# Another cyclic order of the first layer's work on five engines of a fused two-layer attention kernel

## What is computed

```python
x = x + _L0_xattn_ref(_layernorm(x), ctx_1024, ...)  # 16 heads of 8
x = x + _L0_ffn_ref(_layernorm(x), ...)  # 8 experts, top 2
x = x + _L1_xattn_ref(_layernorm(x), ctx_1024, ...)  # 16 heads of 64
x = x + _L1_ffn_ref(_layernorm(x), ...)
```

## Time and profile before

| | us |
|---|---|
| median of 3 runs | 1002.3 (1001.92 to 1004.87) |
| time of the profiled execution | 1007.77 |
| its span, first to last instruction | 1006.1 |
| PE busy (matmuls) | 918.5 (91%) |
| DVE busy | 670.3 (67%) |
| ACT busy | 580.7 (58%) |
| mean granted TensorE clock | 0.962 |

### The profile page before, as it was taken

How to read it: one execution, slowest core, us unless ns; L and a number is a source line. 1 busy time by engine, 2 the same in 40 slices (tenths; PEclk the granted TensorE clock), 3 DMA queues, 4 the chain that set the end, 5 groups by cost and what they waited for, 6 DMA issues and landing times. The chain is left out here.

```text
span 1006.1 us, 30348 instructions
## 1 busy us (share of the span) xinstructions
PE 918.5 (91%) x8590; PEld 800.9 (80%) x8590; DVE 670.3 (67%) x2173; ACT 580.7 (58%) x2537; POOL 414.3 (41%) x670
## 2 busy tenths in 40 slices
PE   4989989899899729999948999999999999999986
PEld 2667767677677529999947899999999999999976
DVE  5778979898699742222226777777777777777763
ACT  1978979899699603332305565556555555555552
POOL 4123434344344421111134555555555555555441
PEclk9999999999899959999978999999999999999998
DMA  4685576756667122222211111111121111111110
GB/s 151 208 247 160 192 228 195 231 191 206 188 197 222 61 69 68 73 68 68 73 55 39 53 54 46 63 57 48 51 63 57 51 48 63 57 43 56 60 48 9
DMA packets 110659, 103.58 MB, mean 103 GB/s; under 512 B 11759, under 2 KB 96563, under 8 KB 110614
## 3 DMA queue, kind: packets, MB, share of 16 engines
q1 hardware_dynamic: 102958, 89.14, 28.5%
q0 software_dynamic: 5776, 12.99, 4.1%
q10 hardware_dynamic: 1880, 0.92, 0.3%
HBM read 56.45 MB, written 46.56 MB: 102 GB/s over the span
## 5 line engine op out<-in xcount | busy, mean ns | idle before, releaser
L590 ACT ACTIVATE PR<-bank,nmx 128x128 f32<-128x128 f32 x1024 | 363.5, 384 | 114.6 <-issue 109.2
L590 ACT ACTIVATION_READ_ACCUMULATOR PR<-bank,nmx 128x1 f32 x1024 | 229.4, 224 | 0.0
L757 DVE TENSOR_REDUCE nmx<-bank 128x4 f32<-128x512 f32 x256 | 168.7, 680 | 35.6 <-PE bank L1051 28.1
L328 POOL TENSOR_TENSOR PR<-PR,rden 128x512 f32<-128x512 f32 x128 | 133.8, 1045 | 88.9 <-DVE rden L762 87.9
L1033 PEld LDWEIGHTS bank<-ident,PR 128*128 128x128 f32 x1024 | 119.9, 142 | 42.8 <-issue 39.4
L1033 PE MATMUL bank<-ident,PR 128*128 128x128 f32 x1024 | 150.1, 277 | 1.0 <-DVE YT L768 1.0
L1212 PE MATMUL bank<-XCT,wqk 128*128 128x128 f32 x1024 | 123.6, 280 | 0.9 <-ACT XCT L582 0.9
L1212 PEld LDWEIGHTS bank<-XCT,wqk 128*128 128x128 f32 x1024 | 120.4, 197 | 1.6 <-ACT XCT L582 1.6
L658 ACT ACTIVATE H<-bank 128x512 f32<-128x512 f32 x70 | 41.8, 597 | 107.0 <-PE bank L1182 107.0
L288 POOL TENSOR_SCALAR veps<-mv 128x1 f32<-128x1 f32 x128 | 28.6, 223 | 181.7 <-DVE mv L304 167.2
L582 ACT ACTIVATE XCT<-bank 128x256 f32<-128x256 f32 x64 | 24.6, 384 | 128.0 <-PE bank L1025 127.7
(11 more groups left out here) (180 smaller groups left out, 1834.1 us busy)
## 6 DMA issues: line engine op xcount, KB each, us to landing
second_layer_values<-wide SPq DMA_DIRECT2D x32, 512.0 KB, 3.3
wide<-second_layer_values SPq DMA_DIRECT2D x32, 512.0 KB, 3.3
expert_outputs<-HF SPq DMA_DIRECT2D x32, 256.0 KB, 2.6
expert_outputs<-HF SPq DMA_DIRECT2D x64, 128.0 KB, 1.9
KBD<-expert_outputs SPq DMA_DIRECT2D x128, 64.0 KB
QS<-expert_outputs SPq DMA_DIRECT2D x32, 256.0 KB
PR<-expert_inputs SPq DMA_DIRECT2D x36, 128.0 KB, 2.0
expert_outputs<-PR POOLq DMA_DIRECT2D x35, 128.0 KB, 2.0
```

The costliest lines, as they stand in the source:

```text
L328: nc.gpsimd.tensor_tensor(unit, unit, rden[:, p, G * g:G * g + G].unsqueeze(2).broadcast_to([P, G, P]), ALU.mult).then_inc(s["nm"], 1)
L590: last = nc.scalar.activation(PR[:, g, j * P:(j + 1) * P], S_BANK[g % 2][:, j * P:(j + 1) * P], ACT.Exp, bias=nmx[:, p, h:h + 1], accum_ou ...
L757: nc.vector.tensor_reduce(nmx[:, p, G * g:G * g + G], S_BANK[g % 2][:].rearrange("p (j k) -> p j k", j=G), AXX, ALU.max, negate=True).then ...
```

## The change

The same instructions are issued in another cyclic order on PE, DVE and ACT, two swaps are made on SP and POOL, and each step is cut at another place, so that late loads and the ends of the pipeline fall elsewhere. With both orders written from V on, in the old numbering of n:

- **PE before**: V(n-2), T1(n-1), transpose of n-3, T2(n-1), o(n-2), S0(n), v0(n), cnt(n-4), transpose of n+2, S1(n), pj0(n+1), T3(n-1), KQ(n+2), RB(n-1), lg(n-3), S2(n), pj1(n+1), T0(n), S3(n).
- **PE after**: V(n-2), S0(n), transpose of n-3, T1(n-1), o(n-2), v0(n), pj0(n+1), S1(n), transpose of n+2, T2(n-1), cnt(n-4), T3(n-1), S2(n), KQ(n+2), RB(n-1), pj1(n+1), T0(n), lg(n-3), S3(n). Its step is now cut ahead of T3, and two more steps are unrolled at the start (`behind` 6 for 4).
- **DVE before**: chosen, ql(n+1), XDT, stats(n+3), x(n-2), reciprocal, M0(n), place and next, M1(n), P2(n-1), stats(n-2), picked, slots, lgs, max, placed, KC to QC(n+2), M2(n), max_index, norm(n-2), tope and hot, M3(n), P0(n), norm(n+3), oN(n-1).
- **DVE after**: ql(n+1), M0(n), XDT, reciprocal, chosen, x(n-2), stats(n-2), stats(n+3), M1(n), place and next, P2(n-1), picked, M2(n), KC to QC(n+2), slots, norm(n+3), placed, lgs, norm(n-2), max, M3(n), max_index to hot, P0(n), oN(n-1).
- **ACT before**: copy of n+2, E0(n), pjv0(n+1), E1(n), P3(n-1), pjv1(n+1), RTS(n-1), E2(n), qh(n+2), E3(n), P1(n), copy vc(n+1).
- **ACT after**: E0(n), copy of n+2, vc(n), pjv0(n+1), E1(n), P3(n-1), E2(n), RTS(n-1), qh(n+2), pjv1(n+1), E3(n), P1(n).
- **SP before**: context(n+3), KBD(n+1), QS(n+1), kw(n+2), store of values(n+1), qw(n+2); loads between loops come ahead of context(n+3).
- **SP after**: QS(n), kw(n+1), store of values(n), context(n+3), early loads, qw(n+1), KBD(n+1); loads between loops come ahead of QS(n). In the cycle only the context and early loads have moved, from behind qw to ahead of it; the late loads have moved from ahead of context and KBD to between KBD and QS.
- **POOL**: the copy XK of n-3 goes behind the two norms.

```diff
@@ -393,32 +393,32 @@
 
             def step0(n, p):
                 q = 1 - p
+                if exists(n):
+                    wait_apart(sp, (a["qw"], 32 * (n + 1)), (a["s"], NU * (n - 1)))
+                    sp.dma_start(QS[:, p, :, :].bitcast(FP32),
+                                 spread(p, 0).rearrange("(g x) s -> x g s", g=NU)).then_inc(a["qs"], 16)
+                if exists(n + 1):
+                    wait_apart(sp, (a["kl"], n + 2), (a["bd"], 16 * G * (n)))
+                    sp.dma_start(spread(q, 1).rearrange("(c o i) s -> c o i s", o=2, i=2),
+                                 PARTS[:, 0:2, :].unsqueeze(1).broadcast_to([P, 2, 2, P])).then_inc(a["kw"], 16)
+                if exists(n):
+                    wait_apart(sp, (a["pjv"], 2 * (n + 1)))
+                    sp.dma_start(v_dram[n], V_OUT).then_inc(a["vst"], 16)
                 if exists(n + 3):
                     load_ctx(sp, a, n + 3, q)
                 if isinstance(n, int):
                     early_loads(n)
                 if exists(n + 1):
+                    wait_apart(sp, (a["ql"], n + 2), (a["qs"], 16 * (n)))
+                    for o in range(2):
+                        sp.dma_start(spread(q, 0).rearrange("(c o i) s -> o c i s", o=2, i=2)[o],
+                                     PARTS[:, 2 + o, :].unsqueeze(1).broadcast_to([P, 2, P])).then_inc(a["qw"], 16)
                     if isinstance(n, int) and n + 1 < 2:
                         sp.wait_ge(bd_zeroed, n + 2)
                     wait_apart(sp, (a["kw"], 16 * (n + 2)), (a["s"], NU * (n)))
                     for j in range(G):
                         rows = spread(q, 1).rearrange("(g j x) s -> j x g s", g=NU, j=G)[j]
                         sp.dma_start(KBD[32 * j:32 * j + 32, q, :, j, :].bitcast(FP32), rows).then_inc(a["bd"], 16)
-                    wait_apart(sp, (a["qw"], 32 * (n + 2)), (a["s"], NU * (n)))
-                    sp.dma_start(QS[:, q, :, :].bitcast(FP32),
-                                 spread(q, 0).rearrange("(g x) s -> x g s", g=NU)).then_inc(a["qs"], 16)
-                if exists(n + 2):
-                    wait_apart(sp, (a["kl"], n + 3), (a["bd"], 16 * G * (n + 1)))
-                    sp.dma_start(spread(p, 1).rearrange("(c o i) s -> c o i s", o=2, i=2),
-                                 PARTS[:, 0:2, :].unsqueeze(1).broadcast_to([P, 2, 2, P])).then_inc(a["kw"], 16)
-                if exists(n + 1):
-                    wait_apart(sp, (a["pjv"], 2 * (n + 2)))
-                    sp.dma_start(v_dram[n + 1], V_OUT).then_inc(a["vst"], 16)
-                if exists(n + 2):
-                    wait_apart(sp, (a["ql"], n + 3), (a["qs"], 16 * (n + 1)))
-                    for o in range(2):
-                        sp.dma_start(spread(p, 0).rearrange("(c o i) s -> o c i s", o=2, i=2)[o],
-                                     PARTS[:, 2 + o, :].unsqueeze(1).broadcast_to([P, 2, P])).then_inc(a["qw"], 16)
                 if isinstance(n, int) and n == -2:
                     sp.wait_ge(rows_zeroed, 1)
                     sp.wait_ge(parts_ready, 1)
@@ -518,15 +518,15 @@
                     nc.gpsimd.tensor_copy(RB[:].rearrange("p (t k d) -> p k t d", t=2, k=PAIRS),
                                           rden[:, q, :].rearrange("p (k t) -> p k t", k=PAIRS).unsqueeze(3)
                                           .broadcast_to([P, PAIRS, 2, DH0])).then_inc(a["rb"], 1)
-                if exists(n - 3):
-                    wait_apart(pool, (rt["xn"], n - 2), *([(rt[f"sc{q}"], 2 * loads(n - 5, q))] if exists(n - 5) else []))
-                    nc.gpsimd.tensor_copy(XK[:, q, :], XND[:]).then_inc(rt["kept"], 1)
                 if exists(n - 2):
                     norm_pool(pool, rt, n - 2, p)
                 if exists(n + 3):
                     norm_pool(pool, a, n + 3, q)
                 if isinstance(n, int):
                     late_constants(n)
+                if exists(n - 3):
+                    wait_apart(pool, (rt["xn"], n - 2), *([(rt[f"sc{q}"], 2 * loads(n - 5, q))] if exists(n - 5) else []))
+                    nc.gpsimd.tensor_copy(XK[:, q, :], XND[:]).then_inc(rt["kept"], 1)
                 if exists(n - 4):
                     for k in range(2):
                         wait_apart(pool, (rt["placed"], n - 3), (rt["kept"], n - 3))
@@ -606,36 +606,36 @@
 
             def step0(n, p):
                 q = 1 - p
+                if exists(n + 1):
+                    act.wait_ge(a["qc"], n + 2)
+                    wait(act, a["qw"], 32 * (n + 1))
+                    nc.scalar.activation(PARTS[:, 2, :].bitcast(FP32R), QC, ACT.Copy).then_inc(a["qh"], 1)
+                if exists(n):
+                    read_v_half(n, 1)
+                if exists(n - 1):
+                    exponentials(a, n - 1, q, 3)
+                    read_PT(a, n - 1, 1)
...
+                if exists(n):
+                    exponentials(a, n, p, 0)
                 if exists(n + 2):
                     read_xct(a, n + 2, p, True, a["v0"], n + 1)
                 if exists(n):
-                    exponentials(a, n, p, 0)
+                    act.wait_ge(a["v0"], n + 1)
...
+                    nc.scalar.activation(diagonal(p), bank[4][:, 2 * P:3 * P].rearrange("p (k t d) -> p k t d", k=PAIRS, t=2),
+                                         ACT.Copy).then_inc(a["vc"], 1)
                 if exists(n + 1):
                     read_v_half(n + 1, 0)
                 if exists(n):
                     exponentials(a, n, p, 1)
                 if exists(n - 1):
                     read_PT(a, n - 1, 3)
-                if exists(n + 1):
-                    read_v_half(n + 1, 1)
+                if exists(n):
+                    exponentials(a, n, p, 2)
                 if exists(n - 1):
                     act.wait_ge(a["rt"], n)
                     wait(act, a["oN"], n - 1)
                     nc.scalar.activation(RTS[:], M2_BANK[:, 2 * P:3 * P], ACT.Copy).then_inc(a["rts"], 1)
-                if exists(n):
-                    exponentials(a, n, p, 2)
-                if exists(n + 2):
-                    act.wait_ge(a["qc"], n + 3)
...
-                    nc.scalar.activation(PARTS[:, 2, :].bitcast(FP32R), QC, ACT.Copy).then_inc(a["qh"], 1)
-                if exists(n):
-                    exponentials(a, n, p, 3)
-                    read_PT(a, n, 1)
-                if exists(n + 1):
-                    act.wait_ge(a["v0"], n + 2)
...
-                    nc.scalar.activation(diagonal(q), bank[4][:, 2 * P:3 * P].rearrange("p (k t d) -> p k t d", k=PAIRS, t=2),
-                                         ACT.Copy).then_inc(a["vc"], 1)
             over_steps(act, step0, -3, NB + 3, 3, 4)
@@ -772,55 +772,63 @@
                 q = 1 - p
                 if isinstance(n, int):
                     weights_and_masks(n)
+                if exists(n - 1):
+                    row_max(a, n - 1, q, 3)
                 if exists(n - 4):
-                    wait(dve, rt["hot"], n - 3)
-                    nc.vector.tensor_tensor(chosen[:], hot1[:, 0, :], hot1[:, 1, :], ALU.add).then_inc(rt["chosen"], 1)
...
+                    wait_apart(dve, (rt["top8"], n - 3))
+                    nc.vector.max_index(topi[:], top8[:], lgs[:]).then_inc(rt["topi"], 1)
...
+                if exists(n - 1):
+                    read_PT(a, n - 1, 0)
+                if exists(n - 2):
...
+                    nc.vector.tensor_tensor(OT0[:, p, :], O_BANK, RTS[:], ALU.mult).then_inc(a["oN"], 1)
+                if exists(n):
+                    row_max(a, n, p, 0)
+                if exists(n - 1):
+                    nc.vector.reciprocal(rden[:, q, :], den[:, q, :]).then_inc(a["rd"], 1)
+                if exists(n - 4):
+                    wait(dve, rt["hot"], n - 3)
+                    nc.vector.tensor_tensor(chosen[:], hot1[:, 0, :], hot1[:, 1, :], ALU.add).then_inc(rt["chosen"], 1)
+                if exists(n - 2):
+                    nc.vector.tensor_tensor(xrow, M2_BANK[:, 0:P], xrow, ALU.add).then_inc(a["x"], 1)
+                    norm_alone_stats(dve, rt, a["x"], n - 2)
                 if exists(n + 3):
                     norm_dve_stats(dve, a, None, n + 3, q)
-                if exists(n - 2):
-                    nc.vector.tensor_tensor(xrow, M2_BANK[:, 0:P], xrow, ALU.add).then_inc(a["x"], 1)
-                if exists(n - 1):
-                if exists(n):
-                    row_max(a, n, p, 0)
+                if exists(n):
+                    row_max(a, n, p, 1)
...
-                if exists(n):
-                    row_max(a, n, p, 1)
-                if exists(n - 2):
-                    norm_alone_stats(dve, rt, a["x"], n - 2)
...
-                    nc.vector.tensor_reduce(slot_f[:, :, bass.ds(n - 4, 1)].rearrange("p k o -> p (k o)"), picked[:], AXX,
...
-                    dve.wait_ge(rt["lg"], n - 2)
-                    nc.vector.tensor_copy(lgs[:], M_BANK[:, 0:NE]).then_inc(rt["lgc"], 1)
```

(89 more changed lines are left out.)

91 lines of the change are left out of this document (42 added, 49 removed).

## The result

The change makes the kernel slower: 1014.2 us median of 4 runs (1010.2 to 1016.8) against 1002.1 (1001.5 to 1004.9), a ratio of 1.0112 with a 95% interval of 1.0072 to 1.0152. A second comparison in another group of runs gave 1.0065 (1.0037 to 1.0094), so in these two the size lies between 0.4 and 1.5%. The sign is plain. My forecast of 994.9 and its range, 987 to 1005, missed. The profiled execution took 1013.0 (span 1011.4), so 5.3 more than that of before.

What follows compares the result with a forecast made beforehand. It took a 9.37 us loop through PE and DVE, both nearly full with ACT, plus four weight-load stalls as the bound. Steady step -5.4, loads 0, start -2.0 gave -7.4: 994.9 us from the 1002.3 median, range 987 to 1005.

Steps and rivals of the forecast that it cites:

- the one on the weight loads: Stalled steps of the first layer and those behind them: gains and losses cancel, sum 0 us, ends -6 and +8.
- QS lands 1.4 us sooner, as KBD no longer waits behind the loads: SP's queue at the stalls: loads start 1.9 us later, half of 7.4 us goes; -1.4 taken.
- M0 behind ql makes the same landing cost 1.1 us more: DVE at the stalls: M0 follows ql at once, so the same landing of QS lengthens a step by 1.1 us.
- k = 4 is too small to stall: The weight load k = 4 in the first layer: expected to cause no stalled step.
- The steps behind the stalls, +1 against -1.1: Steps after the stalls: each 0.27 us shorter, but PE idles 0.5 to 2 us longer before; +1 against -1.1.
- rival 1: Weight loads keep their landing, moving KBD gains nothing, more steps at 1.2 GHz: -1.2 us in all, 1001; chance 0.13.
- The steady step: Undisturbed step of the first layer: 9.37 to 9.1 us, -0.27 for each of 20 steps, -5.4 us.
- The start: First QS lands sooner as bias rows move from between qw(0) and KBD(0): -2.0 us, ends 0 and -4.
- ACT: Undisturbed step: ACT is no bound; its 8.85 us busy in 9.37 is overstated by overlapping durations.
- POOL: Copy XK behind the norms costs nothing, as POOL is busy only 4.15 of 9.37 us.
- the end: End of the layer keeps its dependent chain: 0 us.
- rival 3: QS comes late in every step, S0 waits, steps of 9.7 us: slower, 1011; chance 0.11.

Runs made afterwards that it cites:

- e15: The kernel of e8 run once more; 988.1 us, ratio 0.9841 to the kernel before.
- e9: Kernel after with SP's step cut behind the read of QS and late loads in 13 pieces of about 0.5 MB; 979.6 us, ratio 0.9766.
- e12: Kernel before with only SP's step taken from the kernel after; 1009.1 us, ratio 1.0053 to the kernel before.
- e14: Kernel after run once more, unedited; 1010.7 us, ratio 1.0065 to the kernel before.
- e10: As e9, with POOL's indirect scatter DMAs replaced by plain stores to fixed rows; 981.6 us, ratio 0.9789 to the kernel before.
- e11: As e8, with POOL's indirect scatter DMAs replaced by plain stores to fixed rows; 987.3 us, ratio 0.9844 to the kernel before.
- e3: Kernel after with late loads, except the last rows of X, behind the first layer's last step; 1024.1 us, ratio 1.0023 to the kernel before.
- e4: Kernel before with late loads, except the last rows of X, behind the first layer's last step; 1012.6 us, ratio 0.9896 to the kernel before.
- e8: Kernel before with SP's step cut behind the read of QS and late loads in 13 pieces of about 0.5 MB; 1005.8 us, ratio 0.9869.
- e2: Kernel after with SP's step cut between qw and KBD, so late loads stand ahead of KBD; 1035.9 us, ratio 1.0135 to the kernel before.

## Why the prediction was wrong

**The step that failed is the one on the weight loads.** It read "Sum: 0 us, ends -6 and +8". Like for like, in the two traces: +6.1 for the four stalled steps, +2.5 for the four behind them, +0.7 for k = 4, which is **+9.3 us**. Held against the versions with small pieces, from S0(0) to S0(31), the loads cost 19.6 us before (311.1 against 291.5 in e15) and 30.8 after (315.7 against 284.9 in e9), **11.2 us** between them. In medians it is more: the loads cost before 1 - 0.9841 = 1.6%, and after 1.0065 - 0.9766 = 3.0% (3.5% by the first comparison), so 14 to 19 us between them. Its terms:

- *QS lands 1.4 us sooner, as KBD no longer waits behind the loads.* This is the term that carried the zero, and it was wrong: e12 has the landing 0.25 us later behind qw in the mean. Of "1.9 - 3.7" the 1.9, for loads that start later, was right (2.3 in the mean). The 3.7 was half of the 7.4 us between QS's issue and S0, as if KBD and QS alone filled them; it measured 2.0 in the mean and 1.6 at k = 3.
- *M0 behind ql makes the same landing cost 1.1 us more.* Right. For k = 1 to 3 qw is now issued 1.13 us behind the S0 before it; in before and e12 it was issued 0.16 ahead of it. With the same SP, after's stalled steps exceed e12's by 0.2, 0.7, 1.6 and 1.2, mean 0.9; the steady step is 0.15 shorter, which leaves 1.1.
- *k = 4 is too small to stall.* Wrong: 10.08 us, and 9.8 in e14. The row in after names ACT, but S0(28) needs only E2(27), which ended at 307.8; in e14 the wait at the same place, 0.7 us, is put down to QS. That the 1.1 had used up the slack is my reading.

```profile
310.11 0.38 PE L1049 MATMUL bank<-mk_rows,ones 128*128 128x512 bf16 x1 [0.94 <-ACT PR L590]
```

- *The steps behind the stalls, +1 against -1.1.* Wrong: +2.5, from k = 1 and above all k = 2, where PE now idled 4.6 us before S0 and not 2.5, and the clock fell. At k = 3 it was low for no longer than before (0.77 in 11.62 us, 0.75 in 11.80 before). The steps behind k = 2, before and after:

```profile
197.31:206.47 9.16, 9.10 (x79) 7.11 (x79) 7.87 (x31) 8.03 (x40) 3.93 (x7) 1.00 0.59 194
```

```profile
187.74:198.84 11.10, 11.10 (x78) 8.50 (x78) 7.76 (x32) 7.63 (x36) 3.11 (x7) 0.81 0.39 122
```

This was in the main rival 1, and the signs that I named for it came in part: stalled steps of 13.7 to 15.8 us where I had said 14 to 15.5, and a clock behind them of 0.86, 0.79, 0.81 and 0.77 where I had said under 0.8. I gave it 0.13 and priced it at 1001, since I let it take back the landing and 2 us of clock, but neither the 0.6 us that each stall grew by with SP's part alone nor k = 4.

**The steady step was right in direction and half the size.** Expected 9.37 to 9.1, measured 9.22: DVE is the bound. In every second step it runs without any wait; in the other it loses time where its loop turns round:

```profile
215.89 0.16 DVE L861 MAX8 top<-lgs 128x8 f32<-128x8 f32 x1
215.97 0.67 DVE L757 TENSOR_REDUCE nmx<-bank 128x4 f32<-128x512 f32 x1
...
224.74 0.16 DVE L861 MAX8 top<-lgs 128x8 f32<-128x8 f32 x1
225.19 0.69 DVE L757 TENSOR_REDUCE nmx<-bank 128x4 f32<-128x512 f32 x1 [0.29 <-issue]
...
234.33 0.16 DVE L861 MAX8 top<-lgs 128x8 f32<-128x8 f32 x1
```

From max to max it is 8.85 us in one step and 9.59 in the next, 9.22 in the mean. Of the 0.74 between them, 0.37 is at the turn (M3 starts 0.45 behind max instead of 0.08), and 0.34 in three gaps that are 0.1 longer each, behind hot, next and picked, for which the trace names no cause. Without them PE's 9.05 would be the bound. I had left out what the turn of a hardware loop costs, though the steps of before also alternated.

**The start** was right: S0(0) 2.2 us sooner, and by S0(3) 3.5. In e12, with SP's part alone, S0(0) comes at 21.8, so most of it is SP's. Both together, -7.4 in the prediction, came out at -5.7 (e10, e11) and -7.5 (e9 and e15, from the ratios).

**ACT, POOL, the end, rival 3**: nothing in the traces speaks against the zeros, and QS was late in no undisturbed step between S0(4) and S0(31).

So -7 and +14 to +19 instead of -7 and 0. What stays open is the 3 to 8 us between the 11.2 of the traces and the 14 to 19 of the medians (e12 shows the same gap: its median is 5.9 us above the kernel before, its S0(31) comes at 334.6 where before has 334.4). The medians of e9 and e15 were also taken on different chips. Both traces of before are of executions above their median (1007.8 and 1007.4 against 1002.3 and 1004.8), and none shows what a typical one saves.

## What to carry to other kernels

Bulk loads on the queue of a tight exchange over DRAM cost here by their size first: in pieces of 0.5 MB, about what a step's slack held, they were free behind the last read and cost 4 us ahead of it; in pieces of 1 to 2 MB they cost 16 us in one order and 30 to 35 in the other. Price a reordering with the disturbances in it: a tighter cycle gives up the slack that took them up, each saved tenth in the steady step is small beside a stall that grows by one, and the low clock behind it adds to it (2.4 us on top of 6.6 at k = 3). Before you move a DMA issue out from behind a long transfer, look at whether the transfer hides it: KBD's 1.9 us were hidden in before, and in the open they took back what the shorter queue gave. And when you expect a gain from fewer bytes behind a transfer, multiply the time by the rate first, to see whose bytes fill it.

## What the runs showed of the hardware

In the first two groups of runs the completions of V came late once in each step of the first layer, in either order and with no edit as well: in e3 all of 19 steps between 100 and 300 us have it on DVE, and its total there is

```profile
DVE OT L797 <- remote: 22.1, 19, 1.4
```

while the other two groups have none and the kernel before took 1.5 to 1.8% less. It cost e3 some 1.25 us a step (10.48 against 9.22) and e4 about 0.7 (10.05 against 9.37). That the new order has less room for it, with S0 and T1 between V and o and DVE full, is my reading. It comes near POOL's two indirect DMAs in time (245.4 to 247.8 in the step shown of e3), but they stand at the same place in after (225.3 to 227.7), which has no pause; whether they have a part in it is open.

With the late completions and the loads at the end of the layer, the new order takes 1.3% more than the old (1.0023 against 0.9896), where without them and with small pieces it takes 0.8% less (0.9766 against 0.9841). So on a chip of the first kind e8 may well be faster than e9; that was not run.
